# Masked score products of two small attentions moved from the whole array to two 64-row tiles

## The reference, cut to what matters

```python
# causal, layer 0: softplus squared in place of a softmax
scores = einsum('bhqd,bhkd->bhqk', q, k) * hs ** -0.5
p = softplus(scores) ** 2 * causal
attn = p / (sum(p, -1) + 1e-9)
# cross, layer 0 (with a key mask) and layer 1 (with biases): rotary q and k, context as keys
dots = where(mask, einsum('bhqd,bhkd->bhqk', rope(q), rope(k)) * SCALE, neg)
attn = softmax(dots, -1)
# all three
out = einsum('bhqk,bhkd->bhqd', attn, v)      # then a projection, residual and layer norm
```

## Time and profile before

| | |
|---|---|
| median of three runs | 781.58 us |
| profiled execution, span from first to last instruction | 788.8 us (the page gives no other time of it) |
| mean granted TensorE clock of it | 0.869 of full speed |
| PE, PEld busy | 633.0 us (80%), 513.6 us (65%) |
| DVE, ACT, POOL busy | 505.0 us (64%), 381.3 us (48%), 230.7 us (29%) |
| all score products, L330 on PE | 84.2 us (layer 0), 42.3 us (layer 1) |

### The profile page before, as it was taken

How to read it: one execution, slowest core, us unless ns; L and a number is a source line. 1 busy time by engine, 2 the same in 40 slices (tenths; PEclk the granted TensorE clock), 3 DMA queues, 4 the chain that set the end, 5 groups by cost and what they waited for, 6 DMA issues and landing times. The chain is left out here.

```text
span 788.8 us, 12952 instructions
## 1 busy us (share of the span) xinstructions
PE 633.0 (80%) x3779; PEld 513.6 (65%) x3786; DVE 505.0 (64%) x1221; ACT 381.3 (48%) x966; POOL 230.7 (29%) x254
## 2 busy tenths in 40 slices
PE   4898885999999968699889999979999988781006
PEld 3777774777777756467668888868777776430006
DVE  3788983656675745744544444447677676469886
ACT  3778883445444532133235444435455463484615
POOL 3555552323222211356500000014334331005220
PEclk9899996989997958899979999989899797695558
DMA  5400000001000000000000000001010000000001
GB/s 158 160 11 10 10 13 14 21 21 28 24 20 17 0 1 1 0 1 2 1 11 7 11 10 7 17 14 27 20 26 21 19 17 0 1 0 0 0 0 54
DMA packets 30649, 15.29 MB, mean 19 GB/s; under 512 B 18513, under 2 KB 29841, under 8 KB 30610
## 3 DMA queue, kind: packets, MB, share of 16 engines
q1 hardware_dynamic: 30610, 14.82, 6.7%
HBM read 10.09 MB, written 1.05 MB: 14 GB/s over the span
## 5 line engine op out<-in xcount | busy, mean ns | idle before, releaser
L330 PE MATMUL bank<-a_mov,a_stat 128*128 128x256 f32 x256 | 84.2, 459 | 12.0 <-issue 10.2
L514 DVE TENSOR_REDUCE rowmax<-bank 128x8 f32<-128x512 f32 x64 | 44.2, 691 | 62.2 <-PE bank L330 61.4
L330 PEld LDWEIGHTS bank<-a_mov,a_stat 128*128 128x128 f32 x256 | 50.6, 219 | 28.7 <-issue 23.0
L1213 POOL TENSOR_TENSOR e_hid<-e_gated,e_relu 128x512 f32<-128x512 f32 x32 | 40.6, 1270 | 57.0 <-DVE e_gated L1328 56.8
L1088 PEld LDWEIGHTS bank<-body_sb,e_hid 128*128 128x128 f32 x288 | 37.7, 196 | 22.0 <-issue 13.9
L139 POOL TENSOR_TENSOR xb<-X,made_bias 128x128 f32<-128x128 f32 x32 | 14.6, 457 | 117.2 <-DVE r L149 103.8
L1190 ACT ACTIVATE e_relu<-bank 128x512 f32<-128x512 f32 x36 | 21.5, 598 | 54.2 <-PE bank L1066 45.1
L1328 DVE TENSOR_TENSOR e_gated<-e_relu,bank 128x512 f32<-128x512 f32 x32 | 21.9, 686 | 36.6 <-PE bank L1076 22.5
L252 POOL TENSOR_TENSOR a_stat<-qk,head_sb 128x512 f32<-128x512 f32 x32 | 33.3, 1041 | 37.5 <-ACT qk L405 36.3
L330 PE MATMUL bank<-l_mov,l_stat 128*128 128x256 f32 x128 | 42.3, 462 | 2.2 <-POOL l_mov L252 2.0
L469 ACT ACTIVATE oT<-bank 64x64 f32<-64x64 f32 x192 | 41.7, 217 | 4.1 <-PE bank L375 2.0
(11 more groups left out here) (262 smaller groups left out, 1716.3 us busy)
## 6 DMA issues: line engine op xcount, KB each, us to landing
kvT<-in_ctxT SPq DMA_DIRECT2D x64, 64.0 KB, 2.1
xs<-X SPq DMA_DIRECT2D x56, 64.0 KB, 1.9
body_sb<-in_body SPq DMA_DIRECT2D x2, 950.0 KB, 5.1
body_sb<-in_body SPq DMA_DIRECT2D x2, 949.5 KB, 5.2
out<-X SPq DMA_DIRECT2D x4, 256.0 KB, 2.3
X<-in_x SPq DMA_DIRECT2D x1, 896.0 KB, 6.0
mid_sb<-in_mid SPq DMA_DIRECT2D x1, 448.0 KB, 3.6
head_sb<-in_head SPq DMA_DIRECT2D x1, 422.0 KB, 3.2
```

Of the source, the lines that this page charges most:

```text
L330: mm = nc.tensor.matmul(psS[b][:, 256 * half:256 * half + 256], m.stat[:, par, b, 2 * half:2 * half + 2, :], m.mov[:, par, b, :, :], start ...
L514: nc.vector.tensor_reduce(m.rowmax[:, b, :], psS[b][:, :].rearrange("p (x k) -> p x k", k=T), AX.X, ALU.max).then_inc(s[f"max_done{b}"].se ...
L1213: nc.gpsimd.tensor_tensor(m.hid[:, n % DEEP, :], a, m.relu[:, n % DEEP, :], ALU.mult).then_inc(s["hid_ready"], 1)
```

## The change

Each product of the scores now uses 64 of the array's 128 rows. Channels 0 to 63 (heads 0 to 7) are one tile of the array, channels 64 to 127 (heads 8 to 15) the other. POOL makes two moving copies in place of four (`mask_i` has two columns, repeated for both halves of the channels). Bank u now holds the eight heads of half u for both sequences, where bank b held all heads of sequence b. One step `scores` makes all eight products of a tile, half 0 and half 1 in turn, 128 stationary and 128 moving columns each; it waits for both banks to be free. In layer 0's cross attention both mask products come first. The following steps keep their sizes and take the new order of heads; `outputs` finds the values of its heads from the pair of sequence and head group.

The lists change too. In the cross stages PE does `scores` where `scores0` was, and DVE does `maximum1` and `less_maximum1` directly behind `less_maximum0`. In the causal stage PE does `scores` where `scores1` was. ACT's and POOL's lists stay.

```diff
-        def mask_operand(t, par, out, which, mask, done):
+        def mask_operand(t, par, out, which, mask, copies, done):
...
-                mask.unsqueeze(1).unsqueeze(3).broadcast_to([P, SB, 4, T]), ALU.mult).then_inc(s[done].sem, 1)
+                mask.unsqueeze(1).unsqueeze(3).broadcast_to([P, SB, copies, T]), ALU.mult).then_inc(s[done].sem, 1)
...
         def moving(t, par):
-            mask_operand(t, par, m.mov, 0 if causal else 1, m.mask_i, "mov_ready")
+            mask_operand(t, par, m.mov, 0 if causal else 1, m.mask_i, 2, "mov_ready")
...
-        def scores(t, par, b):
+        def scores(t, par):
             wait_before(pe, before, "scores", t)
             wait(pe, s["stat_ready"], t + 1)
             wait(pe, s["mov_ready"], t + 1)
-            wait(pe, s[f"shifted{b}"], t)
+            wait(pe, s["shifted0"], t)
+            wait(pe, s["shifted1"], t)
             if masked:
-                nc.tensor.matmul(psS[b][:, :], m.ones_bf[0:1, :],
...
+                for u in range(2):
+                    nc.tensor.matmul(psS[u][:, :], m.ones_bf[0:1, :],
...
-            for half in range(2):
-                mm = nc.tensor.matmul(psS[b][:, 256 * half:256 * half + 256], m.stat[:, par, b, 2 * half:2 * half + 2, :],
-                                      m.mov[:, par, b, :, :], start=not masked, stop=True, skip_group_check=masked)
-            mm.then_inc(s[f"s_psum{b}"].sem, 1)
+            for b in range(SB):
+                for x in range(2):
+                    for u in range(2):
+                        rows = slice(u * T, u * T + T)
+                        mm = nc.tensor.matmul(
+                            psS[u][:, :].rearrange("p (b i x k) -> p b i x k", b=SB, i=2, x=2)[:, b, :, x, :],
+                            m.stat[rows, par, b, 2 * x:2 * x + 2, :], m.mov[rows, par, b, :, :],
+                            start=not masked, stop=True, skip_group_check=masked)
+                        if b == SB - 1 and x == 1:
+                            mm.then_inc(s[f"s_psum{u}"].sem, 1)
...
             if causal:
-                run(turn, 0), run(scores1, 1), run(project_outputs, 3), run(project, 0), run(outputs0, 2)
-                run(outputs1, 2), run(values, 0), run(scores0, 0), run(turn_outputs, 2)
+                run(turn, 0), run(scores, 1), run(project_outputs, 3), run(project, 0), run(outputs0, 2)
+                run(outputs1, 2), run(values, 0), run(turn_outputs, 2)
             else:
-                run(turn, 0), run(scores0, 1), run(outputs1, 2), run(project, 0), run(scores1, 1), run(turn_probs0, 1)
+                run(turn, 0), run(scores, 1), run(outputs1, 2), run(project, 0), run(turn_probs0, 1)
                 run(values, 0), run(turn_outputs, 2), run(outputs0, 1), run(project_outputs, 2), run(turn_probs1, 1)
...
-                run(maximum0, 1), run(less_maximum0, 1), run(reciprocals, 2), run(rotate, 0), run(normalise, 2)
-                run(variance, 3), run(maximum1, 1), run(less_maximum1, 1), run(apply, 3), run(residual, 2)
+                run(maximum0, 1), run(less_maximum0, 1), run(maximum1, 1), run(less_maximum1, 1), run(reciprocals, 2)
+                run(rotate, 0), run(normalise, 2), run(variance, 3), run(apply, 3), run(residual, 2)
                 run(statistics, 2)
```

More of the change, by code:

```diff
@@ L253, in mask_operand @@
                 out[:, par, :, :, :],
-                m.qk[:, par, which, :].rearrange("p (b k) -> p b k", b=SB).unsqueeze(2).broadcast_to([P, SB, 4, T]),
-                mask.unsqueeze(1).unsqueeze(3).broadcast_to([P, SB, 4, T]), ALU.mult).then_inc(s[done].sem, 1)
+                m.qk[:, par, which, :].rearrange("p (b k) -> p b k", b=SB).unsqueeze(2).broadcast_to([P, SB, copies, T]),
+                mask.unsqueeze(1).unsqueeze(3).broadcast_to([P, SB, copies, T]), ALU.mult).then_inc(s[done].sem, 1)
         def stationary(t, par):
-            mask_operand(t, par, m.stat, 1 if causal else 0, m.mask_ca if causal else m.mask_ac, "stat_ready")
+            mask_operand(t, par, m.stat, 1 if causal else 0, m.mask_ca if causal else m.mask_ac, 4, "stat_ready")
         def moving(t, par):
-            mask_operand(t, par, m.mov, 0 if causal else 1, m.mask_i, "mov_ready")
+            mask_operand(t, par, m.mov, 0 if causal else 1, m.mask_i, 2, "mov_ready")
         def square1(t, par):
@@ L323, in scores @@
             wait(pe, s["mov_ready"], t + 1)
-            wait(pe, s[f"shifted{b}"], t)
+            wait(pe, s["shifted0"], t)
+            wait(pe, s["shifted1"], t)
             if masked:
-                nc.tensor.matmul(psS[b][:, :], m.ones_bf[0:1, :],
-                                 w.mask_row[0:1, bass.ds(t * P + b * T, T)].unsqueeze(1).broadcast_to([1, 8, T]),
-                                 start=True, stop=False, skip_group_check=True)
-            for half in range(2):
-                mm = nc.tensor.matmul(psS[b][:, 256 * half:256 * half + 256], m.stat[:, par, b, 2 * half:2 * half + 2, :],
-                                      m.mov[:, par, b, :, :], start=not masked, stop=True, skip_group_check=masked)
-            mm.then_inc(s[f"s_psum{b}"].sem, 1)
[L334 to L338, removed]
+                for u in range(2):
+                    nc.tensor.matmul(psS[u][:, :], m.ones_bf[0:1, :],
+                                     w.mask_row[0:1, bass.ds(t * P, P)].rearrange("o (b k) -> o b k", b=SB).unsqueeze(2)
+                                     .broadcast_to([1, SB, 4, T]), start=True, stop=False, skip_group_check=True)
+            for b in range(SB):
[8 more added lines that the diff above has]
+                            mm.then_inc(s[f"s_psum{u}"].sem, 1)
         def turn_probs(t, par, b):
@@ L359, in outputs @@
             wait(pe, s[f"prob_ready{b}" if causal else f"pT_ready{b}"], t + 1)
[L360 to L363, removed]
+            for n in range(4):
+                seq, i = n // 2, 2 * b + n % 2
+                lhsT = m.prob[:, par, b, n, :, :] if causal else m.probT[:, b, n, :]
+                at = 36 * (NI * seq + i)
+                mm = nc.tensor.matmul(psO[:, at:at + 36], lhsT, m.vals[:, par, seq, i, :, :, :], start=True, stop=True)
             mm.then_inc(s[f"o_psum{b}"].sem, 1)
@@ L1623, in _ @@
             apply(NC - 1)
-HEAD_COLS = [("ident", P), ("mask_ac", 4), ("mask_ca", 4), ("mask_i", NI), ("causal", T), ("w0_q", D), ("w0_k", D), ("w0_v", D), ("w0_o", D),
+HEAD_COLS = [("ident", P), ("mask_ac", 4), ("mask_ca", 4), ("mask_i", 2), ("causal", T), ("w0_q", D), ("w0_k", D), ("w0_v", D), ("w0_o", D),
              ("w0_bias", D)]
```

18 lines of the change are left out of this document (8 added, 10 removed).

## The result

The changed kernel takes 874.16 us (median of four runs, 861.25 to 879.34) beside 781.30 us for the kernel before: 93 us more by the medians. The ratio, 1.1085 [1.0980, 1.1189], compares fast runs alone (of the changed kernel 873.22 and 861.25 us) and makes it some 85 us; the profiled execution, 879.34 us, is a slower one at much the same clock (0.753 beside 0.757 and 0.759). The forecast was 836 us with a range of 820 to 878. Direction and range held, but the loss is 1.6 to 1.7 times the 54 us of the sum. The profiled execution has a span of 877.5 us (788.8 before) and a mean granted clock of 0.753 (0.869).

What follows compares the result with a forecast made beforehand. A loop of engines waiting for each other, not PE alone, was taken to bound the cross stages. Terms 23.5 (layer 1 cross), 20.0 (layer 0 cross) and 10.4 us (causal) made 53.9, giving 836 us, range 820 to 878.

Steps and rivals of the forecast that it cites:

- DVE's pair: Cross stages: maximum 1 and subtraction 1 now lie in front of `normalise`, adding 1.34 us per tile to the loop.
- `exponential1` waits for the copies: Cross loop: ACT must first copy the outputs, so the fourth piece stays 3.05 us and nothing comes back for the pair.
- The score products: PE, each tile: 16 passes in 1.01 us; first weight load to DVE's start 1.38 us, against 1.25 before in layer 1.
- the 0.10 for entering the 64-row shape: PE, score products: 0.10 us charged for the change of tiling mode, from 0.31 us behind the mask product less 0.22.
- The rival of the queueing halves: Score products: the two halves' passes queue, 0.67 us more in each of 48 tiles, 32 us, 868 us; chance 0.28.
- the term of 10.4 us: Causal stage: all products stand behind `turn`, so the loop closes at 7.28 us against 6.63, 0.65 us more, 16 tiles.
- the 5.90 us from `scale_and_mask0` to `scores1`: Causal loop before the change, over clamp, exponential, logarithm, `copy_values` and `turn`; with 1.38 us it was to make 7.28.
- my rival: Clock: PE's longer pauses lower the granted clock from 0.90 to 0.83, costing 16 us, 852 us; chance 0.14.
- Cross periods: Cross attention tile periods: 9.60 us in layer 1 (from 8.13) and 9.63 us in layer 0 (from 8.38).
- the forecast of 23.5: Layer 1's cross attention: 1.47 us more per tile over 16 tiles, 23.5 us in all.
- The waits of L345 for ACT: Sign in the cross stages: this PE group should still wait for ACT, longer than before.
- PE's busy share: Sign in the cross stages: it should fall; no size given.

Runs made afterwards that it cites:

- e11: Changed kernel plus products nobody reads in PE's waits (six causal, three and three in the cross stages): 817.09 us, 1.0474 of the kernel before.
- e5: e11 with DVE's cross list of the kernel before: 771.10 us, 0.9805 of the kernel before.
- e4: Changed kernel with ACT's `exponential1` directly behind `exponential0` and PE's `turn_probs1` behind `values` in the cross stages: 840.37 us, 1.0712 of the kernel before.
- e7: Changed kernel with DVE's old cross list, causal `scores` between `values` and `turn_outputs`, and each product on all 128 rows: 854.02 us, 1.0844 of the kernel before.
- e1: Kernel before with only the new order of PE's and DVE's lists, whole-array products kept: 858.87 us, 1.0932 of the kernel before.
- e3: Changed kernel plus six products nobody reads (12 passes) per tile in `turn_outputs`, ahead of its wait for `normalise`: 827.71 us, 1.0529 of the kernel before.
- e8: Kernel before plus products nobody reads in PE's waits (three causal, one and two in the cross stages): 771.47 us, 0.9803 of the kernel before.

## Why the prediction was right in direction and wrong in size

- **DVE's pair: right.** Forecast 1.34 us in the loop; 4.25 - 3.01 = 1.24 us in e11 against e5. That `exponential1` waits for the copies was right too (the tile shown of the kernel after, and e4). Over a whole period in layer 0 the order costs 0.87 us and not 1.24; the 0.38 us by which filler holds up `turn_outputs` in e5 and not in e11 (1.01 less 0.63) make up the difference.
- **The score products: right, and the halves don't queue.** Sixteen passes take 1.93 us in the kernel after, and the same sixteen on all rows take 3.48 us in e7, both at the lower level. At the upper one e5 has 1.16 us for all, 0.06 us apart on average. In the trace the two passes of a pair start 0.01 us apart, and the next pair 0.11 us later (0.20 behind the first pair), so a pair takes the time that one pass takes on all rows:

```profile
69.04 0.30 PE L289 MATMUL bank<-head_sb,xs 128*128 128x128 f32 x1 [0.20 <-ACT vals L423]
69.28 1.16 PE L337 MATMUL bank<-a_mov,a_stat 64*128 64x128 f32 x16
70.46 0.69 DVE L504 SCALAR_TENSOR_TENSOR a_score<-bank,head_sb 128x512 f32<-128x512 f32 x1 [0.58 <-PE bank L337]
```

  From the first pass to DVE it is 1.18 us, where the forecast had 1.38 with the 0.10 for entering the 64-row shape. That 0.10 no run shows. The products start 0.24 us behind `turn` in e5 and 0.14 in the earlier trace rows, but in e1 they use the whole array and also start 0.24 us behind it (median of ten tiles). The 0.31 us behind the mask product that I took it from the earlier trace rows says nothing either: in the same stage the second whole-array pass of a step starts 0.32 us behind the first (median), with no change of shape between them. The Trainium skill, "TensorEngine Tiling (Array Packing)", section "Tiling Modes", says that different tiles can load weights and multiply in parallel; the traces agree (1.93 us beside 3.48). The rival of the queueing halves is out.
- **The causal stage: the term of 10.4 us failed.** The loop closes as forecast (`scale_and_mask` waits 0.58 us for the products in the lines above), but it is not longer. I took the 5.90 us from `scale_and_mask0` to `scores1` as a fixed chain, and it isn't one. In e5 `scale_and_mask` starts at 63.88 and the products at 69.28, 5.40 us; with 1.18 us that is 6.58, about the 6.63 us of before. The second clamp, on the way to `copy_values`, starts 2.63 us behind `scale_and_mask0` and takes 1.06 us before, and 2.36 and 0.73 us in e5 (DVE's wait for `project_outputs` in front of `residual` is gone there; why the clamp is shorter the runs don't show). The line of before, which belongs to the tile of the earlier trace rows, and then e5's:

```profile
64.30 1.06 DVE L504 TENSOR_SCALAR a_soft<-a_score 128x512 f32<-128x512 f32 x1
```

```profile
63.88 0.69 DVE L504 SCALAR_TENSOR_TENSOR a_score<-bank,head_sb 128x512 f32<-128x512 f32 x1 [0.64 <-PE bank L337]
...
66.24 0.73 DVE L513 TENSOR_SCALAR a_soft<-a_score 128x512 f32<-128x512 f32 x1
```

  With the clock at 1.00 the same tiles and the same causal list take 100.1 us (e11), less than before; the median period is 6.64 us in both. So at the upper level the term is nothing, and the 24.8 us measured in the kernel after come back with the clock.
- **The clock: the term that the sum lacked.** The sum kept the clock of before, and my rival let it fall to 0.83 and priced that at 16 us, with 0.14. It fell to 0.61 to 0.69. By the filler (e11) the price is some 48 us of the 85 that the ratio gives, most in the causal stage (130.2 to 100.1 us) and in layer 0 (163.3 to 139.3). I took one stretch at 0.83 as the measure, looked for pauses above all behind DVE's four steps, and did not ask what becomes of the clock when PE needs half the time for its products in a loop that other engines hold: the tiles without DVE's new order take the causal clock to 0.62. The measured time lies in the upper part of the range, which was there for halves that queue with some of the clock, and they don't queue; that the range held is in good part luck.
- **Cross periods.** Forecast 9.60 and 9.63 us at the old clock. At full clock layer 0 has 139.3 / 15 = 9.29 us with the shorter last periods, and 9.48 in the median. Layer 1 has 9.03 us in the tile shown of e11, the first of its stage, which has no `rstd` ahead of `exponential1`; three later ones at a clock of 1.00 take 9.13 to 9.22, and the mean is 149.7 / 15 = 9.98 us at 0.87. So both were forecast right in kind and 0.15 to 0.5 us too long. That layer 1's +23.2 us fits the forecast of 23.5 is partly chance, since its clock was 0.69. How much of it is clock the runs don't show, because no filler brought that stage to 1.00 with the new order.
- **Signs of the forecast that failed.** The waits of L345 for ACT did not grow (12.4 us in its two groups before, 12.3 after), and PE's busy share did not fall (80% both times), as passes at the lower level take longer. PE's longer wait lies elsewhere, at `turn_outputs`, for `normalise` (in the cross stages behind DVE's four steps): 37.5 us in the three stages, 8.8 before. Busy time does not tell work from slow work. Before, then after:

```profile
L375 PE MATMUL bank<-head_sb,o 128*128 128x128 f32 x48 | 14.9, 309 | 8.8 <-DVE o L595 8.3
```

```profile
L380 PE MATMUL bank<-head_sb,o 128*128 128x128 f32 x48 | 18.5, 385 | 37.5 <-DVE o L599 37.3
```

## What to carry to other kernels

Here PE's products were made shorter in a stage whose period other engines hold, and the granted clock fell from 0.93 to 0.61, which cost the stage 24.8 us; a smaller piece of PE's work is not a gain until the clock column has been read. Read it by stage before and after, and price every PE step of the loop at both levels. To find out whether a loss is clock or order, put products that nobody reads into PE's waits and run again: what comes back as the granted clock rises is clock. See in the timeline that the filler itself does not stand in the loop, as 0.38 us of it does in e5. Before a step is put in front of another, look for what lies beside it today; DVE's second pair cost nothing where it lay beside ACT's copies, and 1.24 us in front of `normalise`.

## What was not expected of the hardware

- PE was busy for 62 of 70 us in the causal stage after the change, and in the tile shown of layer 1 it waits no longer than 0.35 us at a time (the longest wait is 1.06 us in the causal stage and 1.67 us in many other tiles of layer 1); the clock stood at 0.61 in the one stretch and 0.69 in the other all the same.
- Twelve filler passes per tile made the kernel after some 43 us faster (e3) and six per tile made the kernel before 2% faster (e8).
- Passes of 128 columns on the two tiles follow each other 0.06 us apart on average at the upper level (e5) and 0.12 at the lower (the kernel after); on all rows it is 0.11 and 0.21 (e7).
